# Two attention layers ahead of a transformer block: new ticks for the side work of the attention stream

## The reference

```
h = layernorm(x) * (1 + ca) + sa
h = h + global_attention(rmsnorm(h) * norm1_w)   # 16 heads of 8, 4 KV heads, causal, RoPE, q/k norm
h = h + local_attention(rmsnorm(h) * norm2_w)    # the same with a window of 32
x = x + ga * h
```

## Time and profile before

| | |
|---|---|
| median of three runs | 1300.59 us (1300.21 to 1301.36) |
| the profiled execution | 1301.36 us, span 1299.6 us |
| mean granted TensorE clock | 0.966 |
| TensorE busy | 1189.1 us (92%) |
| VectorE busy | 977.4 us (75%) |
| ScalarE busy | 834.2 us (64%) |
| GpSimd busy | 446.1 us (34%) |

### The profile page before, as it was taken

How to read it: one execution, slowest core, us unless ns; L and a number is a source line. 1 busy time by engine, 2 the same in 40 slices (tenths; PEclk the granted TensorE clock), 3 DMA queues, 4 the chain that set the end, 5 groups by cost and what they waited for, 6 DMA issues and landing times.

```text
span 1299.6 us, 36705 instructions
## 1 busy us (share of the span) xinstructions
PE 1189.1 (92%) x15602; PEld 674.9 (52%) x15602; DVE 977.4 (75%) x1556; ACT 834.2 (64%) x1229; POOL 446.1 (34%) x582
## 2 busy tenths in 40 slices
PE   4498999999999999688999999999999999999985
PEld 3233334343434455355666666666666666666652
DVE  7878686877759777685787787778777877787755
ACT  3498898888997876445555655565566555645641
POOL 1213211120206457654533433333333333333310
PEclk8599999999999999888999999999999999999997
DMA  3113121021213331101211110011010101101102
GB/s 103 33 28 128 52 84 34 18 98 34 83 34 131 131 115 51 48 18 27 72 27 23 26 27 22 18 29 26 21 27 23 27 22 27 27 23 26 27 6 65
DMA packets 37329, 59.78 MB, mean 46 GB/s; under 512 B 6416, under 2 KB 12464, under 8 KB 37168
## 3 DMA queue, kind: packets, MB, share of 16 engines
q1 hardware_dynamic: 35760, 56.61, 14.8%
q10 hardware_dynamic: 1408, 0.84, 0.3%
HBM read 22.58 MB, written 16.78 MB: 30 GB/s over the span
## 4 chain that ended last, share of the span: by engine, by line
PE 48%; DVE 6%; issue 2%; ACT 1%; POOL 1%; DVEq 0%; POOLq 0%; ACTq 0%
PE psum L1325 9%; PE psum L1461 7%; PE psum L1414 5%; PE psum L1345 5%; PE psum L1436 4%; PE psum L1400 4%; PE psum L1335 4%; PE psum L1487 3%; DVE ffn_neg_max L1810 2%; PE psum L1385 2%; PE psum L1422 1%; PE psum L1391 1%; ACT ffn_hn L1666 1%; PE psum L1453 1%; PE psum L1357 1%
## 5 line engine op out<-in xcount | busy, mean ns | idle before, releaser
L816 ACT ACTIVATE att_probs<-psum 128x1024 f32<-128x1024 f32 (+2 forms) x384 | 356.2, 997 | 63.9 <-PE psum L673 61.3
L1757 POOL TENSOR_TENSOR ffn_rot<-ffn_rot,ffn_rot_sin 128x512 f32<-128x512 f32 x128 | 160.3, 1274 | 385.8 <-DVE ffn_rot L1788 385.8
L717 PE MATMUL psum<-att_probs,att_v 128*32 128x256 f32 (+3 forms) x3712 | 239.9, 347 | 11.8 <-DVE att_probs L1008 7.8
L673 PE MATMUL psum<-att_q_stack,att_k_parts 64*128 64x512 bf16 (+4 forms) x1280 | 148.9, 295 | 13.3 <-DMA att_q_stack<-att_q_low 6.6
L1008 DVE TENSOR_TENSOR att_probs<-att_probs,att_causal_mask 128x1024 f32<-128x1024 f32 (+1 forms) x80 | 96.6, 1220 | 38.8 <-ACT att_probs L816 38.4
L717 PEld LDWEIGHTS psum<-att_probs,att_v 128*32 128x32 f32 x3712 | 77.2, 109 | 88.8 <-issue 67.8
L1639 ACT ACTIVATE ffn_max_t<-psum 68x128 bf16<-68x128 bf16 x64 | 17.4, 273 | 152.3 <-PE psum L1373 152.0
L673 PEld LDWEIGHTS psum<-att_q_stack,att_k_parts 64*128 64x128 bf16 x1280 | 44.8, 94 | 132.9 <-ACT att_probs L816 70.1
L1646 ACT ACTIVATE ffn_probs<-psum 128x1024 f32<-128x1024 f32 x64 | 65.7, 1026 | 59.2 <-PE psum L1400 59.2
L585 POOL TENSOR_TENSOR att_probs<-att_probs,att_local_mask 128x480 f32<-128x480 f32 (+1 forms) x48 | 62.8, 1315 | 91.0 <-ACT att_probs L816 90.8
L1608 ACT ACTIVATE ffn_sq<-psum 128x512 f32<-128x512 f32 x128 | 75.3, 594 | 27.8 <-PE psum L1325 27.7
(11 more groups left out here) (222 smaller groups left out, 2452.1 us busy)
## 6 DMA issues: line engine op xcount, KB each, us to landing
ffn_v_back<-ffn_v SPq DMA_DIRECT2D x120, 130.0 KB, 2.4
att_q_stack<-q_rows SPq DMA_DIRECT2D x28, 512.0 KB, 3.6
q_rows<-att_q_high SPq DMA_DIRECT2D x21, 256.0 KB, 4.5
q_rows<-att_q_mid SPq DMA_DIRECT2D x21, 256.0 KB, 4.3
q_rows<-att_q_low SPq DMA_DIRECT2D x14, 256.0 KB, 4.2
xres<-in_hidden SPq DMA_DIRECT2D x4, 512.0 KB, 5.9
out<-ffn_qk_t SPq DMA_DIRECT2D x3, 512.0 KB, 3.2
tail_f_wqkv<-in_f_wqkv SPq DMA_DIRECT2D x1, 768.0 KB, 4.8
```

Source lines behind the costliest of these rows:

```text
L673: ins = T.matmul(psum[:, banks[i] + at:banks[i] + at + width], k_parts[rows, p % 3, j, kt * P:(kt + 1) * P], q_stack[rows, turn % 2, j, q0 ...
L717: ins = T.matmul(psum[32 * g:32 * g + V_PAD, (4 + cc) * BANK + lo - cc * BANK: (4 + cc) * BANK + hi - cc * BANK], v[:, p % 4, kt, g, shift ...
L816: act.activation(probs[:, n % E_BUFS, 2 * j:2 * j + 2, 0:width], ps2((step % 2) * 2).rearrange("p (h c) -> p h c", h=2)[:, :, 0:width], AC ...
L1757: steps.did(pool.tensor_tensor(out, out, halves(k.rot_sin[:, n % 2, :])[:, :, 1 - half, :], ALU.add), g["added"] if half else None)
```

## The change

Only the tables change. No operation is added or removed, and on TensorE the order of the side jobs stays the same; on VectorE and ScalarE some steps change their place among the others. A few ticks move by one to three, some steps by up to six.

```diff
 OPENS = ((0, 6), (0, 3))
 CLOSES = ((2, 5), (3, 7))
 
-LN_AT = (None, -5, 13, 29)
-QKV_AT = (-12, -3, 32, 54, 81, 101, 128, 152)
-OUT_AT = ((22, 41, 63, 68), (74, 88, 93, 97), (100, 113, 115, 123), (130, 147, 150, 151),
-          (164, 169, 174, 175), (177, 179, 183, 184), (186, 188, 192, 195))
+LN_AT = (None, -5, 15, 26)
+QKV_AT = (-12, 2, 31, 60, 86, 107, 133, 152)
+OUT_AT = ((23, 42, 63, 68), (74, 88, 93, 97), (100, 113, 114, 123), (129, 147, 150, 151),
+          (164, 166, 173, 175), (177, 179, 183, 184), (186, 188, 192, 195))
 POST_AT = (176, 185)
 
 FIRST = dict(square=0, transpose=0, reduce=0, evacuate=1, roots=1, refine=1, project0=2, project1=2, copy0=3, scale0=3,
              copy1=3, scale1=3, head_square=3, cos=3, head_reduce=3, head_roots=4, sin=4, add=4, newton=4, rotate=4,
              q_transpose=5, q_hi=5, k_split=5, q_lo=6, k_transpose=6, k_hi=6, k_lo=6)
 QKV_STEPS = (FIRST,
-             dict(square=0, transpose=8, reduce=9, evacuate=10, roots=11, refine=11, project0=12, copy0=12,
-                  scale0=13, project1=14, copy1=14, scale1=14, head_square=14, cos=16, head_reduce=18, sin=19, add=20,
-                  head_roots=22, newton=23, rotate=23, k_split=23, q_transpose=30, q_hi=30, q_lo=31, k_transpose=33,
-                  k_hi=33, k_lo=33),
-             dict(square=0, transpose=2, reduce=2, evacuate=4, roots=5, refine=5, project0=6, copy0=6, scale0=7,
-                  project1=11, copy1=11, cos=11, head_square=13, scale1=14, head_reduce=17, sin=17, head_roots=17,
-                  newton=17, add=19, rotate=19, k_split=20, q_transpose=22, q_hi=22, q_lo=23, k_transpose=25, k_hi=25,
+             dict(square=0, transpose=3, evacuate=3, reduce=4, roots=6, refine=7, project0=7, copy0=9, scale0=10,
+                  project1=11, copy1=11, scale1=11, head_square=11, cos=12, head_reduce=13, sin=14, add=16,
+                  head_roots=17, newton=17, rotate=18, k_split=20, q_transpose=24, q_hi=24, q_lo=27, k_transpose=28,
+                  k_lo=28, k_hi=29),
+             dict(square=0, transpose=2, reduce=5, evacuate=6, roots=7, project0=8, copy0=8, refine=9, scale0=11,
+                  project1=13, copy1=13, cos=13, scale1=14, head_square=18, head_reduce=18, sin=18, head_roots=18,
+                  newton=18, add=18, rotate=19, k_split=21, q_transpose=23, q_hi=23, q_lo=24, k_transpose=26, k_hi=26,
+                  k_lo=28),
+             dict(square=0, reduce=0, transpose=1, evacuate=1, roots=3, refine=4, project0=6, copy0=6, scale0=7,
+                  project1=10, copy1=10, head_square=10, cos=10, scale1=11, head_reduce=11, sin=11, head_roots=14,
+                  newton=14, add=14, rotate=14, k_split=15, q_transpose=22, q_hi=22, q_lo=23, k_transpose=24, k_hi=24,
                   k_lo=25),
-             dict(square=0, reduce=2, transpose=7, evacuate=7, roots=9, refine=10, project0=12, copy0=12,
-                  scale0=13, project1=16, copy1=16, head_square=16, cos=16, scale1=17, head_reduce=17, sin=19,
-                  head_roots=20, newton=20, add=22, rotate=23, k_split=25, q_transpose=26, q_hi=28, q_lo=29,
-                  k_transpose=30, k_hi=30, k_lo=31),
-             dict(square=0, transpose=5, evacuate=6, reduce=6, roots=8, refine=9, project0=9, copy0=9, scale0=10,
-                  project1=14, copy1=14, scale1=14, head_square=15, cos=15, head_reduce=15, sin=18, head_roots=18,
-                  newton=21, add=21, rotate=22, k_split=23, q_transpose=26, q_hi=26, q_lo=27, k_transpose=28, k_hi=28,
-                  k_lo=28),
-             dict(square=0, transpose=10, evacuate=11, reduce=11, roots=12, refine=13, project0=16, copy0=16,
-                  scale0=17, project1=18, copy1=18, cos=18, scale1=19, head_square=19, head_reduce=19, sin=20, add=20,
-                  head_roots=21, newton=27, rotate=27, k_split=30, q_transpose=31, q_hi=31, q_lo=32, k_transpose=33,
-                  k_hi=33, k_lo=33),
-             dict(square=0, transpose=10, evacuate=10, reduce=11, roots=11, refine=11, project0=12, copy0=12,
-                  scale0=13, project1=15, copy1=15, cos=15, head_square=16, scale1=18, head_reduce=18, sin=20,
-                  head_roots=21, newton=21, add=21, rotate=22, k_split=24, q_transpose=25, q_hi=25, q_lo=27,
-                  k_transpose=28, k_hi=28, k_lo=28),
-             dict(square=0, reduce=4, transpose=6, evacuate=6, roots=7, refine=8, project0=8, copy0=8, scale0=9,
-                  project1=10, copy1=10, scale1=10, head_square=10, cos=10, head_reduce=10, sin=12, head_roots=12,
-                  add=12, newton=14, rotate=15, k_split=18, q_transpose=19, q_hi=19, q_lo=19, k_lo=20, k_transpose=21,
-                  k_hi=21))
+             dict(square=0, transpose=0, evacuate=0, reduce=3, roots=4, refine=4, project0=4, copy0=6, scale0=7,
+                  project1=9, copy1=9, scale1=9, head_square=10, cos=10, head_reduce=10, sin=12, head_roots=13,
+                  newton=14, add=15, rotate=16, k_split=18, q_transpose=21, q_hi=21, q_lo=22, k_transpose=23, k_hi=23,
+                  k_lo=23),
+             dict(square=0, transpose=4, evacuate=6, reduce=6, roots=6, refine=7, project0=8, copy0=8, scale0=9,
+                  project1=12, copy1=12, scale1=12, cos=13, head_square=14, head_reduce=14, sin=16, head_roots=16,
+                  newton=17, add=18, rotate=22, k_split=24, q_transpose=24, q_hi=24, q_lo=25, k_lo=25, k_transpose=27,
+                  k_hi=27),
+             dict(square=0, reduce=4, transpose=5, evacuate=5, roots=6, refine=7, project0=7, copy0=7, scale0=8,
+                  project1=9, copy1=10, cos=10, scale1=11, head_square=11, head_reduce=13, sin=14, add=15,
+                  head_roots=16, newton=16, rotate=17, k_split=19, q_transpose=20, q_hi=21, q_lo=22, k_transpose=23,
+                  k_hi=23, k_lo=23),
+             dict(square=0, transpose=6, evacuate=6, reduce=6, roots=7, refine=8, project0=8, copy0=8, scale0=9,
+                  project1=10, copy1=10, scale1=10, head_square=10, cos=10, head_reduce=11, sin=11, head_roots=12,
+                  add=13, newton=13, rotate=15, k_split=16, q_hi=17, q_transpose=18, q_lo=18, k_lo=19, k_transpose=20,
+                  k_hi=20))
 URGENT = (0, len(PHASES) - 1)
 LN_STEPS = (None, dict(stats=0, roots=1, norm=1, shift=1),
-            dict(stats=0, roots=4, norm=12, shift=19),
-            dict(stats=0, roots=4, norm=4, shift=5))
-POST_STEPS = (dict(gate=0, stats=3, roots=6, norm=6, shift=7, transpose=14, evacuate=14),
-              dict(gate=0, stats=2, roots=4, norm=10, shift=10))
+            dict(stats=0, roots=6, norm=9, shift=12),
+            dict(stats=0, roots=4, norm=4, shift=7))
+POST_STEPS = (dict(gate=0, stats=2, roots=6, norm=6, shift=7, transpose=14, evacuate=14),
+              dict(gate=0, stats=2, roots=5, norm=7, shift=9))
 MODULATE_AT = -10
 FIRST_GATHER_AT = -5
 SUMS_ON_ACT, HEADS_ON_ACT, ROWS_ON_ACT = 8, 3, 6
```

## The result

The changed kernel takes 1309.58 us (median of four runs, 1308.69 to 1310.3) where the kernel before, run beside it, takes 1300.4 (four runs, 1298.43 to 1301.36). The ratio is 1.0073, 95% interval 1.0057 to 1.0088: slower by 9.2 us. The forecast was slower by 3.2, 1303.8, with a range that ended at 1308.0. The sign held; the size did not, and the range ended 1.6 us short of the time.

What follows compares the result with a forecast made beforehand. It took TensorE and ScalarE, both full in the global ticks, as the bound. Terms -1.6 + 0.4 + 0.9 + 0.35 + 2.6 + 0.25 + 0.3 = +3.2 us on the 1300.59 median gave 1303.8 us, range 1297.0 to 1308.0.

Steps and rivals of the forecast that it cites:

- What bounds it: Global ticks, with TensorE and ScalarE both full: time moves by tick length, and nothing changes after the last tick.
- Ticks 9 to 40: Phases 1 and 2 and layernorms: new stops at ticks 19, 30 and 32, less crowding at 38; -1.6 us.
- the crowd at 38: Tick 38, 6.5 us long before: `evacuate` would end at 139.9, before `project0` wants it at 140.3, so the crowd goes.
- a low clock as a rival: Half clock after each 2 us stop (ticks 30, 75, 170), 1.7 us each: 1308.9 us; chance 0.1, within the slower case.
- Ticks 71 to 86: Phase 3: stop at tick 75 grows to 1.95 us, 0.8 at tick 82, transposes save 0.2; +0.9 us (0 to 1.5).
- Ticks 40 to 71: `project1` and `cos` of phase 2 one tick later delay `head_reduce` some 0.3 us; +0.4 us (0 to 0.6).
- Ticks 86 to 111: Phase 4: `close1` at tick 93 waits 0.9 us for `scale0`, other moves partly offset; +0.35 us (-0.3 to 1.2).
- Ticks 111 to 138: TensorE jobs one tick after jobs VectorE must read: 0.7 at 114, 0.5 at 115, 0.9 at 131; +2.6 us (1 to 3.5).
- Ticks 138 to 176: Phase 6 `copy1` +0.25; phase 7 waits of 1.9 and 2.1 us replace 4.15 us of old waits, +0.3 (-1.5 to 2).
- VectorE is earlier than laid out: Rival: VectorE 2 us earlier removes most stops at ticks 19, 30, 32, 75, 82 and 93; 1295.6 us, chance 0.23.
- The moves cancel: Rival: stops only wander between ticks, so the time stays within 0.2%, 1300.6 us; chance 0.31.

Runs made afterwards that it cites:

- x1: g1 with `q_lo` of phase 1 back ahead of the mask product of tick 28 and `k_hi` from tick 31 to 30: 1298.49 us, ratio 0.9989.
- x2: g1 with the layernorm of batch 3 back at its old ticks, `stats` behind unit 29: 1303.05 us, ratio 1.0023.
- y1: The whole changed kernel with `q_lo` of phase 1 ahead of tick 28's mask product and `k_hi` at 30: 1305.61 us, ratio 1.0046.
- g1: The kernel before with only the new layernorm ticks and steps, phases 1 and 2 and output of phase 0: 1303.87 us, ratio 1.0034.
- g2: The kernel before with only the new ticks of phase 3: 1301.98 us, ratio 1.0018.
- x3: g2 with only `sin` of phase 3 put back to tick 73, behind that tick's product: 1303.58 us, ratio 1.0024.
- y2: g2 with `add`, `rotate` and `k_split` of phase 3 put back to ticks 76, 77 and 79, `sin` left: 1300.61 us, ratio 1.0002.
- y3: g3 with jobs on neighbouring ticks apart again (`close2` 115, `project0` 117, `open0` 130, `q_transpose` 132): 1302.37 us, ratio 1.0018.
- g3: The kernel before with only the new phases 4 and 5 and outputs of phases 2 and 3: 1304.68 us, ratio 1.0035.
- g4: The kernel before with only the new phases 6 and 7, output of phase 4 and layernorms after the attention: 1299.83 us, ratio 0.9996.
- w2: g4 plus `norm` of batch 2 behind unit 29's product, `stats` of batch 3 at 30, adjusted new phase 2, `refine` at 39: 1298.03 us, ratio 0.9977.
- w1: As w2 but `refine` of phase 2 at 40, behind `scale0`, which leaves out the right scaling (timing only): 1297.42 us, ratio 0.9974.

## Why the prediction was right in its sign and wrong in its size

- **What bounds it.** Right: the global ticks took the loss, and the way behind the last tick didn't change.
- **Ticks 9 to 40, the step that failed.** The prediction said "`q_lo` comes after unit 28 and not before; unit 29 is late by 1.6 us at tick 32". It asked who of VectorE's own products comes late from the new order, and not who waits for `q_lo` itself. That is `k_transpose` of the next tick, through the side banks, the same dependence that I priced at 114, 115 and 131. It waits 2.84 us. The stops that were laid out came: 0.83 us at tick 19 (0.9), 1.68 at tick 30 (2.2), and the crowd at 38 is gone (2.3 us instead of 6.5). The stop at tick 32 for unit 29 (1.6) didn't come: TensorE was late itself by the wait of L771. Those of 0.75 us at tick 20 and of 0.58 us at tick 26, for the sums, were not forecast. Shown by `x1` (-5.4 us), `x2` and `y1` (-4.0).
- **Its clock.** I priced a low clock as a rival for single stops of 2 us, 1.7 us for each. At tick 30 two stops follow each other, and the low stretch is 10.2 us long (6.8 in `g1`, with the same length of tick). In `x1` and `y1`, without the long wait, there is none. Between `g1` and `x1` the waits fell by 2.8 us and grew by 1.2 elsewhere, 1.6 in sum, while the ticks 9 to 40 differ by 4.6 us in the two traces. The other 3.0 us go with the 6.8 us at 0.50 that `g1` had and `x1` has not: most of the price of that wait was clock, in these traces.
- **Ticks 71 to 86, a term of the wrong size.** The stop at 75 is right (1.95, measured 2.02). That at 82 was laid out with the old duration of `add`, 1.49 us. In its new place it meets GpSimd's square and takes 3.07. (The square's own tick went from 81 to 86, but GpSimd runs ahead of its ticks and still does it right behind `newton`.) By these rows: 0.8 + 1.6 = 2.4, measured 2.11 us. The low clock behind it is the rest: without one there `g2`, `x3` and `y1` have +2.1 in these ticks, 1.3 less than the changed kernel. I had used the collision for tick 30 and left it out here. `x3` and `y2` show that `sin` has no part in it.
- **Ticks 40 to 71** cost 0.0 where I took 0.4: the later `head_reduce` was hidden.
- **Ticks 86 to 111** right in place: the wait at 93 is 1.30 us (0.9), the sum 0.7 (0.35).
- **Ticks 111 to 138** right in place and size: 0.77 us at 114 (0.7), 0.56 at 115 (0.5), 0.43 at 122 (0.6), 0.55 at 131 (0.9), sum 2.7 (2.6). `y3` takes 2.4 of the 2.8 us of `g3` back.
- **Ticks 138 to 176** right: 1.29 and 1.75 us in phase 7 (1.9 and 2.1) in place of the old waits; `g4` is at 0.9996. The measured +1.0 holds a stretch of 3.4 us at the lower clock behind the stop of tick 170. It is no clear cost of the change: in the same ticks of `g1`, `g2` and `g3`, where nothing of them is changed, such a stretch follows the stop of tick 152 and is worth +1.1 to +1.2, and the profile before and `y3`, which has 0.0, are those without one.
- **The rivals.** "VectorE is earlier than laid out" is wrong: the stops at 19, 30, 75, 82 and 93 all came. "The moves cancel" is wrong. That of the clock has the direction: of its three ticks, stretches followed at 30 and 170, none at 75, and one at 82, which it didn't name. Where no stop behind them shrank in return, such stretches cost 1.1 to 1.5 us each, not 1.7. But it knew neither the second wait of tick 30, which kept TensorE from its work, nor the second stop of tick 82.

Put together: the 6.9 us between the forecast for the ticks (+3.2) and the measured +10.1 are 3.6 in ticks 9 to 40, 2.5 in ticks 71 to 86, and 0.8 in the others. For the first part the failed step is shown by runs. For the second the size of the stop is worked out from the rows, and that the three moved steps cause it is shown by `y2`.

The Trainium skill, page SBUF — State Buffer, section "Who interferes with whom", says besides that a VectorE operation with at most one SBUF input, outside the two-port modes, doesn't contend with GpSimd. The rows agree: the statistics beside GpSimd's `shift` took 1.63 us in `w2`, where `x2` has 1.64 for them with GpSimd idle, while a mask product, with two inputs, took 2.87 beside `shift` in `x1` and 0.69 alone in `y2`. By that rule `stats` is the operation to put beside `shift`. One input alone is not enough, though: L1144, right behind `stats`, has one SBUF input too and was held up for 2.08 us in `w2`. In which mode it ran no view shows.

## What to carry to other kernels

When a step is moved on an in-order engine, list for each operation that it issues who waits for it, and through which buffer: a wait for a buffer to come free can stand in the profile without a releaser ("issue"), as at the ticks 30 and 93 here, and it can be the longest of all. Use the duration that an operation has beside its new neighbours, not its old one. And first try the parts one at a time: here four of them added up to the whole, and the place of one step held some two fifths of it.

## What the runs showed of the hardware

- **A stop doesn't always draw the lower clock.** The ticks up to 70 are the same in seven of the kernels profiled (before, `g2`, `g3`, `g4`, `x3`, `y2`, `y3`). The stop of 3.1 us at tick 31 was followed by 3.4 us at 0.50 in all seven, the crowd at tick 38 in three (before, `g2`, `x3`). The stop of 2.0 to 2.1 us at tick 75 drew one in `g2` and `y1`, and none in the changed kernel and `y2`; one of 2.48 us at tick 82 of `x3` drew none. The stop of 2.1 us at tick 152 was followed by one in seven of the nine profiles that have the old tables of the phases 6 and 7 (not in before and `y3`); the stops of 1.29 and 1.75 us at the ticks 169 and 170 in four of the five with the new ones (not in `w1`). Equal ticks differ by up to 1.6 us between two profiles for this reason (ticks 9 to 40 of `g4` against those of before: -1.5).
- **The same two stops, another low stretch, the same price.** At tick 30 `g1` has both stops too (1.68 and 3.28 us), and 6.8 us at 0.50 from 121.7 us on, within the second stop. The changed kernel has 10.2 us from 119.4 on, right behind the first. Tick 30 takes 9.42 us in both, since most of the first 3.4 us lay beside the wait for `q_lo`. Why one stretch began earlier stays open. The first stop alone, the same 1.68 us, was followed by none in `x1` and `y1`.
- **A tiny operation can be held up as long as a big one**: L1144, 8 elements a partition, took 2.08 us beside GpSimd's `shift` instead of 0.17.
